# Attention B of a hybrid layer: softmax exponentials transposed by VectorE and DMA in place of TensorE, with the scores seven pairs ahead

## The reference

```python
q = jnp.einsum('bim,mhd->bhid', x, wq)
k = jnp.einsum('bim,mhd->bhid', x, wk)
v = jnp.einsum('bim,mhd->bhid', x, wv)
q = rope(q)
k = rope(k)
s = jnp.einsum('bhid,bhjd->bhij', q * mult, k * mult)
mask = jnp.less(i, j)                      # causal
s = s - INFTY_APPROX * mask
p = jax.nn.softmax(s, axis=-1)
o = jnp.einsum('bhij,bhjd->bhid', p, v)
r = jnp.einsum('bhid,hdm->bim', o, wo)
...
x = x + _L0_attn_b_ref(_layernorm(x, axis=-1), wq, wk, wv, wo)
```

## Time and profile before

| | before |
|---|---|
| time, median of 3 runs | 1645.89 us (1645.23 to 1647.15) |
| the profiled execution: its time, its span | 1645.33 us, 1643.5 us |
| mean granted clock of TensorE over the span | 0.98 |
| TensorE / VectorE / ScalarE / GpSimd busy, share of the span | 95% / 64% / 53% / 38% |
| attention B, from its first to its last matmul of lines 950 to 977 | 771.9 to 1340.5 us |
| transposes of the exponentials on TensorE (line 960) | 384, 272 to 333 ns each |
| copies of them by ScalarE (line 1094) | 128, median 478 ns |

### The profile page before, as it was taken

The page is one execution under the profiler, slowest core; times in us unless marked ns, Lnnn a source line. Parts: engine busy times, 40 slices in busy tenths (PEclk is TensorE's granted clock), DMA queues, the critical chain, the costliest instruction groups (busy, mean ns, idle before and its releaser), DMA issues. The chain is left out here.

```text
span 1643.5 us, 29373 instructions
## 1 busy us (share of the span) xinstructions
PE 1559.3 (95%) x9784; PEld 1351.8 (82%) x9784; DVE 1052.8 (64%) x2464; ACT 867.6 (53%) x2140; POOL 631.3 (38%) x550
## 2 busy tenths in 40 slices
PE   6699999999789999996999999999999969999998
PEld 4588888888678888885888989998998967888887
DVE  6577777777775555565566566666656677555554
ACT  3366666666543333324777767767767734323332
POOL 2676777767300000004656656655655610000000
PEclk9799999999989999997999999999999989999999
DMA  2100000000010000001000000000000001000001
GB/s 94 54 16 17 17 16 15 16 0 1 1 65 20 20 20 19 0 1 58 7 20 8 26 19 7 19 7 19 14 19 0 1 1 39 20 20 20 19 1 52
DMA packets 10654, 32.41 MB, mean 20 GB/s; under 512 B 1088, under 2 KB 5184, under 8 KB 10560
## 3 DMA queue, kind: packets, MB, share of 16 engines
q1 hardware_dynamic: 10560, 31.28, 5.6%
HBM read 29.18 MB, written 2.10 MB: 19 GB/s over the span
## 5 line engine op out<-in xcount | busy, mean ns | idle before, releaser
L378 POOL TENSOR_TENSOR ab_swapped<-ab_swapped,const 128x512 f32<-128x512 f32 x128 | 167.4, 1308 | 224.5 <-DVE ab_qk L378 154.2
L1466 ACT ACTIVATE f_silu<-ps 128x512 f32<-128x512 f32 x128 | 76.3, 598 | 283.0 <-PE ps L116 282.9
L1576 DVE TENSOR_TENSOR f_hidden<-ps,f_silu 128x512 f32<-128x512 f32 x128 | 87.7, 690 | 201.9 <-PE ps L116 201.9
L114 PE MATMUL ps<-xh,f_wl 128*128 128x512 f32 x512 | 203.2, 397 | 1.5 <-DVE f_hidden L1576 1.5
L115 PE MATMUL ps<-xl,f_wh 128*128 128x512 f32 x512 | 202.8, 396 | 0.0
L116 PE MATMUL ps<-xh,f_wh 128*128 128x512 f32 x512 | 202.6, 396 | 0.0
L1203 DVE SCALAR_TENSOR_TENSOR x<-ps,ab_inv,x 128x256 f32<-128x256 f32 x256 | 123.3, 483 | 84.5 <-PE ps L116 79.9
L1295 POOL TENSOR_TENSOR ab_qk<-ab_qk,ab_swapped 128x512 f32<-128x512 f32 x128 | 167.4, 1308 | 10.0
L73 POOL TENSOR_TENSOR rstd<-shifted,minus_half 128x4 f32<-128x4 f32 x16 | 17.0, 1066 | 350.0 <-DVE shifted L67 350.0
L626 ACT ACTIVATE aa_probs<-ps,aa_negmax 128x256 f32<-128x256 f32 x256 | 119.3, 473 | 60.7 <-DVE aa_negmax L709 53.3
L114 PE MATMUL ps<-f_wh,f_hl 128*128 128x256 f32 x512 | 144.4, 282 | 3.3 <-DVE x L1592 3.3
(11 more groups left out here) (189 smaller groups left out, 4606.8 us busy)
## 6 DMA issues: line engine op xcount, KB each, us to landing
f_stage<-wf_in SPq DMA_DIRECT2D x16, 768.0 KB, 4.2
b_stage<-wb_qkv_in SPq DMA_DIRECT2D x8, 768.0 KB, 4.3
a_stage<-wa_in SPq DMA_DIRECT2D x8, 608.0 KB, 3.8
x<-x_in SPq DMA_DIRECT2D x4, 512.0 KB, 6.9
bo_stage<-wb_out_in SPq DMA_DIRECT2D x8, 256.0 KB, 2.6
out<-x SPq DMA_DIRECT2D x4, 512.0 KB, 2.9
const<-const_in SPq DMA_DIRECT2D x1, 704.0 KB, 5.2
open_small_in<-small_weights SPq DMA_DIRECT2D x1, 392.0 KB, 6.7
```

What stands on the lines that cost most here:

```text
L114: nc.tensor.matmul(out, ll, rh, start=start, stop=False)
L378: return engine.tensor_tensor(by_batch(out), by_batch(src), table(c, rows, col), ALU.mult)
L1576: nc.vector.tensor_tensor(hidden[:, m, :], UP(m), silu[:, m, :], ALU.mult).then_inc(hid_done, 1)
```

## The change

`turn`, `take_turned` and bank 2 are gone. In their place VectorE transposes all of a pair's exponentials at once, in squares of 32x32, into `squares` (`turn_squares`); such a square stays in its 32 partitions, so for each slot 16 DMAs from SyncE's queue bring the squares to their partitions in `probsT` (`move_squares`, 48 KB each, 32 partitions x 1536 bytes). `mix` reads `probsT` in runs of 32 columns. Scores, maxima and exponentials run seven pairs ahead in place of two, the projections two and three slots ahead, and the split of part 0 comes at s = 1, j = 1 in place of s = 2.

```diff
-    W = T + P
+    W, SQ, LEAD = T + P, 32, 7
+    LANDED = 16 * 16
...
+            def move_squares(n):
+                sp.wait_ge(squares_done, PAIRS * (n + 1))
+                after(sp, pv_done, PAIRS * (n - 1))
+                for qs in range(4):
+                    for ks in range(4):
+                        sp.dma_start(probsT[ks * SQ:(ks + 1) * SQ, n % 2, qs], squares[qs * SQ:(qs + 1) * SQ, n % 2, ks]).then_inc(landed[n % 2], 16)
...
             def project_values(it, s, i):
-                pe.wait_ge(rope_read, 4 * n + 3 + i)
-                pe.wait_ge(swap_done, 4 * n + 3 + i)
+                before = (4 * n + 7, 4 * n + 10)[i]
+                pe.wait_ge(rope_read, before)
+                pe.wait_ge(swap_done, before)
...
-            def turn(it, s, j):
-                pe.wait_ge(exp_done, g + 1)
-                after(pe, probsT_done, g)
-                for i in range(3):
-                    ins = nc.tensor.transpose(TURN[:, i * P:(i + 1) * P], probs[:, j, i * P:(i + 1) * P], c.ident)
...
             def mix(it, s, j):
-                pe.wait_ge(probsT_done, g + 1)
                 if j == 0:
+                    pe.wait_ge(landed[s % 2], LANDED * (2 * it + s // 2 + 1))
...
+                columns = lambda kinds: probsT[:, s % 2, :, kinds, j, :].rearrange("p a k i -> p k a i")
...
             def step(it, s, j):                                   # TensorE
-                    scores(*moved(it, s, j, 2))
-                turn(it, s, j)
+                if exists(it, s, j, LEAD):
+                    scores(*moved(it, s, j, LEAD))
                 if not (first and s == 0 and j == 0):
                     mix(*moved(it, s, j, -1))
-                if j == 0 and not (last and s == NG - 1):
-                    project(*nxt, 2)
-                    project(*nxt, 3)
-                if j in (1, 2) and not (last and s == NG - 1):
-                    project_values(*nxt, j - 1)
+                if j == 0 and not (last and s >= NG - 2):
+                    project(*moved(it, s, 0, 2 * PAIRS)[:2], 2)
+                    project(*moved(it, s, 0, 2 * PAIRS)[:2], 3)
+                if j in (1, 3) and not (last and s == NG - 1):
+                    project_values(*moved(it, s, 0, PAIRS)[:2], j // 2)
                 if j >= 2 and not (first and s == 0):
                     output(*moved(it, s, 0, -PAIRS)[:2], j - 2)
                 if j == 0 and not (first and s <= 1):
                     output(*moved(it, s, 0, -2 * PAIRS)[:2], 3)
-                if j == 3 and not (last and s >= NG - 2):
-                    project(*moved(it, s, 0, 2 * PAIRS)[:2], 0)
-                    project(*moved(it, s, 0, 2 * PAIRS)[:2], 1)
+                if j == 2 and not (last and s >= 1):
+                    project(*moved(it, s, 0, 3 * PAIRS)[:2], 0)
+                    project(*moved(it, s, 0, 3 * PAIRS)[:2], 1)
                 if j == 3 and not (first and s == 0):
                     output(*moved(it, s, 0, -PAIRS)[:2], 2)
...
             def step(it, s, j):                                   # ScalarE
-                take_turned(it, s, j)
+                if s == 1 and j == 1 and not last:
+                    split_hi(it + 1, 0)
+                if exists(it, s, j, LEAD):
+                    exps(*moved(it, s, j, LEAD))
...
+            def turn_squares(it, s, j):
+                after(dve, landed[s % 2], LANDED * (2 * it + s // 2))
+                nc.vector.transpose(out=squares[:, s % 2, :, :, j, :], in_=probs[:, j].rearrange("p (k b i) -> p b k i", k=3, b=4)).then_inc(squares_done, 1)
...
             def step(it, s, j):                                   # VectorE
+                    row_max(*moved(it, s, j, LEAD))
+                if s == 1 and j == 1 and not last:
+                    split_lo(it + 1, 0)
+                if exists(it, s, j, LEAD - 1):
+                    invert(*moved(it, s, j, LEAD - 1))
+                    turn_squares(*moved(it, s, j, LEAD - 1))
```

More of the change, by code:

```diff
@@ L912, in project @@
                     pe.wait_ge(w_lo, 2 * it + 1)
-                if i >= 2:
-                    pe.wait_ge(rope_read, 4 * n + i - 1)
-                    pe.wait_ge(swap_done, 4 * n + i - 1)
-                else:
-                    after(pe, values_done, 2 * n + i - 1)
+                early = isinstance(n, int) and n < 2
+                if i == 0:
+                    if early:
+                        after(pe, rope_read, 3 * n)
+                        after(pe, swap_done, 3 * n)
+                    else:
+                        pe.wait_ge(values_done, 2 * n - 3)
+                elif i == 3 and not early:
+                    pe.wait_ge(values_done, 2 * n - 2)
+                else:
+                    before = (0, 4 * n, 4 * n + 1, 4 * n + 2)[i]
+                    after(pe, rope_read, before)
+                    after(pe, swap_done, before)
                 col = slice((i // 2) * P, (i // 2) * P + P)
@@ L1028, in head_pair @@
                         step(it, s, j)
[L1030 to L1033, removed]
+            for i in range(4):
+                project(0, 0, i)
             norm_turn(nc, c, own_norm, pe, 2, own_banks)
-            project_values(0, 0, 0)
-            project_values(0, 0, 1)
-            norm_turn(nc, c, own_norm, pe, 3, own_banks)
             project(0, 1, 0)
@@ L1041, in _ @@
             scores(0, 0, 1)
+            project(0, 1, 2)
+            project(0, 1, 3)
+            scores(0, 0, 2)
+            scores(0, 0, 3)
+            project_values(0, 0, 0)
+            norm_turn(nc, c, own_norm, pe, 3, own_banks)
+            pe.wait_ge(own_norm.lo_done, KD * (NG - 1))
+            project(0, 2, 0)
+            project(0, 2, 1)
+            scores(0, 1, 0)
+            scores(0, 1, 1)
+            project_values(0, 0, 1)
+            scores(0, 1, 2)
             pe.wait_ge(own_norm.lo_done, KD * NG)
@@ L1140, in _ @@
             split_hi(0, 1)
-            swap(0, 0, 0)
-            swap(0, 0, 1)
-            swap(0, 0, 2)
-            swap(0, 0, 3)
+            for i in range(4):
+                swap(0, 0, i)
             norm_hi(nc, c, own_norm, act, 2, own_banks)
-            take_values(0, 0, 0)
-            take_values(0, 0, 1)
-            norm_hi(nc, c, own_norm, act, 3, own_banks)
             swap(0, 1, 0)
@@ L1152, in _ @@
             exps(0, 0, 1)
+            swap(0, 1, 2)
+            swap(0, 1, 3)
+            exps(0, 0, 2)
+            exps(0, 0, 3)
+            take_values(0, 0, 0)
+            norm_hi(nc, c, own_norm, act, 3, own_banks)
+            swap(0, 2, 0)
+            swap(0, 2, 1)
+            exps(0, 1, 0)
+            exps(0, 1, 1)
+            take_values(0, 0, 1)
+            exps(0, 1, 2)
             head_pair(0)
@@ L1228, in step @@
                         norm_rows(nc, c, norm, dve, s - 2)
-                    if not (last and s >= NG - 2):
-                        rope(*moved(it, s, 0, 2 * PAIRS)[:2], 0)
-                        rope(*moved(it, s, 0, 2 * PAIRS)[:2], 1)
                 if s == 1 and j == 1:
@@ L1262, in _ @@
             row_max(0, 0, 1)
-            invert(0, 0, 0)
+            rope(0, 1, 2)
+            rope(0, 1, 3)
+            for j in range(2):
+                invert(0, 0, j)
+                turn_squares(0, 0, j)
+            row_max(0, 0, 2)
+            row_max(0, 0, 3)
+            norm_lo(nc, c, own_norm, dve, 3, own_banks)
+            rope(0, 2, 0)
+            rope(0, 2, 1)
+            for j in range(2, 4):
+                invert(0, 0, j)
+                turn_squares(0, 0, j)
+            row_max(0, 1, 0)
+            row_max(0, 1, 1)
+            for j in range(2):
+                invert(0, 1, j)
+                turn_squares(0, 1, j)
+            row_max(0, 1, 2)
             for it in range(HP):
```

91 lines of the change are left out of this document (43 added, 48 removed).

## The result

| | before | after |
|---|---|---|
| time, median | 1645.56 us (1643.02 to 1647.15) | 1720.38 us (1717.96 to 1722.58) |
| ratio to before, with its 95% interval | | 1.0452 [1.0439, 1.0465] |
| the profiled execution's span | 1643.5 us | 1719.2 us |
| mean granted clock of TensorE over the span | 0.98 | 0.97 |

The changed kernel is slower by 74.8 us. Forecast were 64 us, 1710 us in all, with a range of 1680 to 1735.

A forecast was written before the change was run, and what follows sets the result against it. TensorE was taken to bound the kernel through the distances between its matmul starts. The terms, -42 + 37 + 30 + 26 + 1 + 11 + 1 = +64 us on 1645.33 us, gave 1710 us, range 1680 to 1735.

The forecast's parts named there:

- transposes off TensorE: Between scores and mix, three transposes costing 0.33 us disappear from TensorE for each of 128 pairs: -42 us.
- wait at the output bank: In j = 3, output(2) directly follows output(1) and waits for add_out(1): 29 x 1.26 = +37 us.
- wait at the projection bank: In j = 3, project_values(1) waits for rope and copies to free bank 4: 29 x 1.02 = +30 us.
- the split, idle: In s = 1, j = 2, output(0) waits 3.7 us behind the weights' split, in seven head pairs: +26 us.
- the clock behind it: After the split's wait, TensorE runs 3.1 us at half speed, losing 1.6 us, seven times: +11 us.
- the eighth head pair: The last head pair has no weights' split and waits about 1 us: +1 us.
- both ends: More projections and scores before the block's first mix, fewer in its last slots: +1 us, between -4 and +5.
- What bounds the kernel: In the steady stretch, distances between TensorE's matmul starts set the time; each new wait costs in full.
- save perhaps the first: Sign to look for: TensorE never waits for a transfer's landing, except perhaps the first; no size given.
- The transposes on VectorE: One per pair at 0.55 us, 2.2 us a slot, hidden in VectorE's 6.8 us free.
- Rival D: Transposes take 1.1 us or more, making mixed_lo late each slot, or mix slows: 1730 to 1780 us; chance 0.08.
- The transfers: SyncE's 16 per slot take 5.3 us of issue plus 4.3 landing, hidden unless an issue costs 0.67 us.

The follow-up runs named there:

- experiment 5: Kernel before, without its transposes and ScalarE's copies of them, mix reading untransposed exponentials (another output): 1611.89 us, ratio 0.9788.
- experiment 4: Kernel before, with only output(2) moved directly behind output(1) in j = 3, ahead of both projections: 1686.53 us, ratio 1.0239.
- experiments 1: Changed kernel, with TensorE's project_values(1) in j = 3 moved between output(1) and output(2): 1656.92 us, ratio 1.0064 to before.
- experiment 2: Changed kernel, with the weights' split_lo moved behind add_out, mixed_lo and split_wo on VectorE in s = 1, j = 1: 1699.01 us, ratio 1.0316 to before.
- 3: Changed kernel with both reorderings, TensorE's outputs set apart and VectorE's split_lo moved behind: 1634.06 us, ratio 0.9924 to before.
- experiment 9: Changed kernel with outputs set apart, plus 12 matmuls nobody reads ahead of output(0) in s = 1, j = 2: 1646.87 us, ratio 1.0008 to before.
- Experiment 7: Changed kernel with both reorderings, without the transfers, mix reading squares in place (another output): 1629.30 us, ratio 0.9896 to before.
- experiment 8: Changed kernel with both reorderings, VectorE transposing each pair a second time into an unread tensor: 1653.82 us, ratio 1.0043 to before.
- experiment 6: Changed kernel with both reorderings, each of a slot's 16 transfers cut in two, 32 of 24 KB: 1772.31 us, ratio 1.0762 to before.
- 10: Changed kernel with both reorderings, plus project(0), project(1) and their ropes moved ahead in j = 2 except s = 1: 1631.66 us, ratio 0.9911 to before.

## Why the prediction was right

Slower, by the mechanism named, inside the range, and by 10.8 us more than forecast. The sum, term by term:

| term | predicted | measured | from |
|---|---|---|---|
| transposes off TensorE | -42 | -42 | 0.33 us at each of 128 places (0.65 us from scores to mix); experiment 5, in the old order, gave -35 |
| wait at the output bank | +37 | +40 | 29 x 1.37 (experiment 4) |
| wait at the projection bank | +30 | +28 | 29 x 0.97 (987.17 to 988.71, less the usual 0.57) |
| the split, idle | +26 | +25 | 24.9 us in seven waits |
| the clock behind it | +11 | +17 | 41.6 - 24.9; 2 of it are no clock, see below |
| the eighth head pair | +1 | 0 | no wait in its step, 3.06 us |
| both ends | +1 | +7 | what is left of 74.8 |

- **What bounds the kernel.** Right: TensorE's distances set the time, so each new wait cost in full, and the effects of experiments 1 and 2 add up in 3.
- **The waits at the banks.** Right to 0.12 us each, the projection bank 0.97 us for 1.02. The chains built from rows of other places in the program held, because they are chains of the same instructions. Missing was the slow first matmul behind a wait, 0.11 us.
- **The split.** The idle time was right, 3.56 us for 3.7, and so was the slowing beside GpSimd: the split takes 2.01 us with GpSimd busy for 1.93 of them, and 1.22 us before with GpSimd idle. The output weights' split shows the same the other way round, 0.68 us here with GpSimd idle for the 1.71 before.
- **The clock.** The step that failed in size: "3.1 us at half speed lose 1.6 us". In five of seven cases the stalled step is 6.5 us too long, of which 3.6 is idle: 2.9 us lost, not 1.6. By experiment 9 the step without half clock is 3.85 us late and not 3.56, so some 2.7 of the 2.9 us are the clock's, and of the term's 17 us 15 are. After TensorE's restart the half clock lasted from 980.31 to 986.0, 5.7 us and not 3.1. One case in the earlier trace rows was too thin a base for a duration. This is half of the error. Experiment 9 shows that this loss comes from the idle time.
- **Both ends.** The other half, +7 us for +1. 4.8 of it is the first mix's wait for the first landing, which the prediction allowed as "save perhaps the first" without a price, and 2.5 the half clock behind that wait (a first step of 5.28 us for 2.73). Experiment 7, in which both are gone, confirms it. So this too is a stall with its clock. The rest of the two ends was not taken apart.
- **The transposes on VectorE.** 0.56 us for 0.55. Hidden, though with less to spare than "6.8 us free" a slot suggests: at 1.1 us each they cost 20 us (experiment 8). Rival D was right in that this would cost, and wrong in how: no wait for `mixed_lo` in each slot, and the price comes through the clock as much as through waits.
- **The transfers.** Hidden as forecast, but with a term off by two: an issue takes 0.68 us, not 0.33, so 10.9 us instead of 5.3. The threshold given, 0.67 us, was put on a window of 15 us and a landing of 4.3; by that threshold the 0.68 us measured would just have been late. It was not, since a landing of 48 KB takes 1.9 us and the window was 17.4 us. That this part came out hidden is partly luck, two errors of opposite sign; experiment 6 shows the edge.
- **The rule on small transfers.** The Trainium skill, page "DMA: Bandwidth & Descriptors", section on the anatomy of one DMA, gives a fixed 2.0 us beside the bytes. That page of the Trainium skill fitted it to DMAs that GpSimd issues; the 1.9 us measured here for SyncE's agree with it. From these figures the prediction worked out 34 us a slot for transfers that run one after the other, beside a rule of the Trainium skill, in the same page's rules for kernel authors, against transfers under 64 KB. They overlap: 16 were through in 12.8 us. The rule of the same page of the Trainium skill to issue early and wait late describes why they cost nothing here.
- **What was not forecast** is that the change is a gain once two orders are mended. The change that was to bring 42 us lost them to three places of order, none of which the transposes need.

## What to carry to other kernels

When a long lead frees an engine, look at what the reordering has put next to each other: two users of one bank, or a once-per-loop task in a queue on which the bound engine waits. Their prices can be worked out beforehand from the distances between the same instructions elsewhere in the trace, and each was mended here by moving one group of instructions.

A stall of TensorE can cost up to 1.8 times its length, through the clock (6.5 us for 3.6 here); if it can't be removed, filling it with matmuls that nobody reads gave back what the clock took in experiment 9.

A hidden resource is known only by its margin: doubling it (experiments 6 and 8) shows how far off its edge is.

## What was not expected of the hardware

- A SyncE issue takes 0.65 us for 24 KB and 0.68 for 48 KB between partitions of SBUF. A weight load's issue takes 0.33 us in kernels without such transfers (before, experiment 7) and 0.58 in those with them. Why was not tried.
- The same wait of 0.44 and 1.26 us at the same place was followed by half clock in two of seven cases (experiment 2), in none (3), in one (10), in two (7), and with 0.8 in place of 0.44 us in four (8), each in one profiled execution. What decides between the cases stays open.
- An fp32 transpose of 128x384 in squares of 32x32 takes 0.56 us, and a matmul operand read in runs of 32 columns costs no more than a contiguous one.
